# A four-layer graph network kernel: in its second layer, 20 edge tiles of a group are gathered and 5 go by counts, in place of 15 and 10

## The reference, cut to what matters

```python
def _L1_gnn_ref(features, src, dst, W, b):
    out_deg = segment_sum(ones, src); in_deg = segment_sum(ones, dst)
    ci = rsqrt(maximum(out_deg, 1.0)); cj = rsqrt(maximum(in_deg, 1.0))
    msg = features[src] * ci[src][:, None]
    agg = segment_sum(msg, dst) * cj[:, None]
    h = where(in_deg[:, None] > 0, agg, features)
    return relu(h @ W.T + b)
```

## Time and profile before

| | us |
|---|---|
| median of 3 runs | 16802.36 (16799.04 to 16803.32) |
| the profiled execution | 16791.52 |
| its span | 16789.7 |
| `pass1`, from its first body on DVE to its last add | 4280.6 to 7713.2 |
| DVE / POOL / PE busy from 4280 to 7720 | 2392 / 1794 / 2243 of 3440 |
| ACT busy there | 784 |

### The profile page before, as it was taken

How to read it: one execution, slowest core, us unless ns; L and a number is a source line. 1 busy time by engine, 2 the same in 40 slices (tenths; PEclk the granted TensorE clock), 3 DMA queues, 4 the chain that set the end, 5 groups by cost and what they waited for, 6 DMA issues and landing times. The chain is left out here.

```text
span 16789.7 us, 290124 instructions
## 1 busy us (share of the span) xinstructions
PE 11513.4 (69%) x64352; PEld 9568.8 (57%) x64353; DVE 8750.1 (52%) x19588; ACT 3873.3 (23%) x10408; POOL 11073.3 (66%) x11400
## 2 busy tenths in 40 slices
PE   7877877877666666665777766666755446666666
PEld 6777777777444444444555666566643336565555
DVE  4666666666677666664111444444432234444444
ACT  1111111111222222223444211111022223333331
POOL 4777777777545555555666777777546777777773
PEclk9999999999766666665555555555555555555555
DMA  5444444443111111112333333333223333333331
GB/s 130 101 101 101 101 100 101 102 101 91 47 40 43 45 46 44 46 44 76 110 110 110 95 87 87 86 84 90 71 77 92 94 92 95 88 96 92 92 92 51
DMA packets 1579142, 1406.93 MB, mean 84 GB/s; under 512 B 987004, under 2 KB 1445903, under 8 KB 1574658
## 3 DMA queue, kind: packets, MB, share of 16 engines
q1 hardware_dynamic: 601532, 636.68, 14.5%
q0 software_dynamic: 410000, 462.80, 11.0%
q10 hardware_dynamic: 567508, 306.27, 6.6%
HBM read 984.49 MB, written 420.17 MB: 84 GB/s over the span
## 5 line engine op out<-in xcount | busy, mean ns | idle before, releaser
L1757 POOL DMA_INDIRECT order<-l_msg,l_uring x6250 | 6069.5, 971 | 2356.7 <-issue 1831.9
L547 POOL DMA_INDIRECT l_rows<-btab,l_sd x3125 | 2993.7, 958 | 1128.3 <-issue 1087.2
L1906 PEld LDWEIGHTS ps<-l_ordb,l_ohs 128*128 128x128 f32 x15040 | 3263.7, 331 | 313.8 <-issue 313.8
L1906 PE MATMUL ps<-l_ordb,l_ohs 128*128 128x49 f32 x15040 | 3385.3, 415 | 0.0
L1086 POOL DMA_INDIRECT l_rows<-y,l_sd x1875 | 1822.0, 972 | 1621.5 <-DMA l_sd<-in_sd 1087.9
L688 PE MATMUL ps<-l_rhs,l_lhs 64*128 x6250 | 1421.9, 424 | 666.5 <-DVE l_rows L624 466.5
L688 PEld LDWEIGHTS ps<-l_rhs,l_lhs 64*128 64x128 f32 x6250 | 1350.8, 328 | 728.1 <-issue 728.1
L1904 PE MATMUL ps<-l_none 1*128 1x490 bf16 x752 | 438.0, 582 | 1694.4 <-DVE l_ohs L1789 1143.1
L1071 ACT ACTIVATE l_adj<-ps 128x588 f16<-128x588 f32 x1260 | 784.0, 664 | 2636.3 <-PE ps L1315 2629.0
L703 PEld LDWEIGHTS ps<-l_ohe,l_hid 128*128 128x128 f32 x6250 | 1342.8, 332 | 34.7 <-issue 34.0
L703 PE MATMUL ps<-l_ohe,l_hid 128*128 128x32 f32 x6250 | 1359.8, 402 | 0.6 <-ACT l_hid L733 0.6
(11 more groups left out here) (317 smaller groups left out, 15842.4 us busy)
## 6 DMA issues: line engine op xcount, KB each, us to landing
l_ordb<-order SPq DMA_DIRECT2D x752, 250.0 KB
l_dstb<-ids SPq DMA_DIRECT2D x250, 600.0 KB
order<-l_msg,l_uring POOLq DMA_INDIRECT x6250
order<-l_zero ACTq DMA_DIRECT2D x125, 775.0 KB
l_eat<-in_ea40P SPq DMA_DIRECT2D x625, 120.0 KB, 2.1
gates<-l_made ACTq DMA_DIRECT2D x625, 120.0 KB
l_gin<-gates SPq DMA_DIRECT2D x125, 600.0 KB
l_rows<-btab,l_sd POOLq DMA_INDIRECT x3125
```

What stands on the lines that cost most here:

```text
L547: pool.indirect_dma_start(rows[:, t, :], None, d["btab"], bass.IndirectOffsetOnAxis(ap=sd[:, t, 0:1], axis=0)).then_inc(gat[c], 16)
L1757: pool.indirect_dma_start(d["order"], bass.IndirectOffsetOnAxis(ap=uring[:, t:t + 1], axis=0), msg[:, t, :], None).then_inc(sc[c], 16)
L1906: done = t.matmul(red[b % 2][:, ds(slots[k], MW)], ohs[b][:, k, :], ordb[b][:, k, 0:MW], start=False, stop=False, skip_group_check=True)
```

## The change

`SC` goes from 3 to 4, so 20 tiles are gathered and 5 go by counts. The one-hots and builds are laid out anew around the ranking steps: 3 tiles, then the other 2.

```diff
-SC = 3
+SC = 4
 ST = SC * CT
 DT = GT - ST
...
-                    one_hots(0, 4)
+                    one_hots(0, 3)
                     blocks(0)
                     blocks(1)
-                    one_hots(4, 7)
+                    one_hots(3, DT)
                     counts(0)
                     blocks(2)
-                    one_hots(7, 10)
                     counts(1)
                     add_sums(w)
                     blocks(3)
...
-                    build(0, 4)
+                    build(0, 3)
                     before_chunk(0)
-                    build(4, 7)
+                    build(3, DT)
                     behind_chunk(0)
                     before_chunk(1)
-                    build(7, DT)
                     behind_chunk(1)
                     before_chunk(2)
```

## The result

The changed kernel takes 16500.24 us (median of 4 runs, 16497.71 to 16502.51). The ratio to the kernel before is 0.9822, with a 95% interval of 0.9807 to 0.9838: 1.8% faster and clear of no change, as forecast, 23 us under the 16523 and inside the range. The profiled execution took 16502.51 us, against 16791.52 before: -289, where the steps gave -279.

A forecast was written before the change was run, and what follows sets the result against it. The DVE-TensorE chain bounded `pass1`; POOL's gathers would take over. 39 groups at 25.4 us and 84 at 25.35 gave -279 us, 16512.5, plus 10.8 to the median: 16523 us, range 16490 to 16625.

The forecast's parts named there:

- the steps: Summed terms for `pass1`: TensorE's end -277.6 us, four adds behind it -1.1, together -279 us.
- The bound: In `pass1`, POOL's gathers, hidden so far, become the bound: 25.35 us a group against a chain of 24.5 in the last 85.
- The body: Group 17's second body in `pass1` goes, 125 bodies in place of 126: 22.4 us less in the chain.
- The gathers: Twenty gathers a group on POOL, 0.952 us at the median plus 0.305 gap each, taken as 25.35 us a group.
- Landing: From the last gather's end to the use of its rows on TensorE at the end of `pass1`: about 2 us, an estimate.
- The chain: DVE with a piece of TensorE behind the adds: 2.5 us less a body, 27.9 to 25.4 and 27.0 to 24.5.
- the layout: New order of one-hots, builds and count steps: `counts(1)` starts at 5.2 us, not 4.6; wait of 0.6 to 0.7 us.
- the register loads: Five registers fewer for DVE to load at a group's start: gain between 0 and 0.65 us, taken as 0.
- adds and `ohe`: DVE steps in each body: 9 adds in place of 13, -1.13 us; `ohe` of 640 elements, not 480, +0.19 us.
- The columns: `multiply` on TensorE moves half the columns, but weight loads set its spacing of 0.08 us: no gain, -0.
- The two fp32 rows: First-layer 32-column and later-layer 49-column matmuls, same weights, 0.213 and 0.215 us each; taken to show weight loads set the spacing.
- the rival: DVE blocks POOL's gathers: gain eaten at 27.6 us a group; at 29.5 us, 231 us later, 17033 us; chance 3%.

The follow-up runs named there:

- the first eight experiments: Changed kernel: one gather more, five fewer, one DVE step, two fp32 steps; kernel before: five gathers more, one body less, half columns, more register loads; 16400.87 to 16851.39 us.
- the kernel with 15: Kernel before (15 gathers a group) with one further DVE comparison a body, on the slower chip: 24174.59 us, ratio 1.0033 to the kernel before there.

## Why the prediction was right

**The bound.** The chain of DVE and a piece of TensorE, 27 us, gave way to POOL, as laid out: a full gather's price arrives at the end (+157 us), five gathers fewer give back 112 us, and a DVE step gives 9 in place of 84.

**The body.** -22.4 was read, -24.5 measured.

**The gathers.** 25.35 us a group were put; the first wait behind which they run through is at 4308.29 and the last ends at 7416.1, so (7416.1 - 4308.3) / 123 = 25.27. The wait came 2 us later than put (4306.3). 123 x 0.1 = 12 us less and 2 more are the 10 us by which the last gather is early. The mean gather took 959 ns, with fewer one-hots on DVE beside it. Landing took 1.46 us where I estimated 2.

**The chain.** Its saving was mis-sized. I had 2.5 us a body, for 25.4 us in the first 40 groups and 24.5 behind them. The chain by itself, in the changed kernel with 15 gathers, takes 24.4 and 24.0, so 3.5 and 3.0 are saved. One-hots, adds and the layout came out within 0.1 us of the steps (5.19 for 5.2, 5.78 for 5.9, 2.55 for 9 x 0.282). The term that failed is the register loads, "I take 0": 0.50 us of the bound of 0.65. That accounts for the 3.0 behind the first 40 groups. The further 0.5 us within them lie in two other terms. Taken group by group from the traces of before and of the kernel with 15 gathers (groups 2 to 37 without 17), the way from the first one-hot to the first add fell from 7.62 to 5.73 us, 1.9 in place of the 1.6 put, so TensorE showed through with 0.36 us and not 0.65; and the way from there to the reduce fell from 9.69 to 8.64 us, 1.05 where adds and `ohe` had been put at 0.94. It did not move the end, since POOL binds at 25.3 either way; it shows only in how soon POOL has spent its lead: the first 40 groups run at 24.8 us, faster than the gathers, from the lead that they begin with.

**The columns.** -0 was right, by the trace and by the experiment with half the columns. The 0.08 us is the spacing at a granted clock of 0.50 and not at every clock (0.045 us at 1.00). The two fp32 rows could not bear the conclusion: they differ in columns (32 and 49) but also in the granted clock, 1.00 at 1999.74 and 0.50 at 10008.45. Only the experiment changes the columns alone.

**The sum to the median.** The kernel before's profiled execution lay 10.8 us under its median, and I carried that over; after, it lay 2.3 us above. Of the 23 us by which the forecast was high, 13 are this offset and 10 the gathers.

**DVE and the gathers.** That DVE's steps would not make the gathers the slower way was right on the chips of the first eight experiments: their mean stayed at 959 ns. The reading under it was too weak, though. I had "0.2 us and not more" for what a step can cost a gather, while the earlier trace rows already has one of 1325 ns, and the changed kernel has gathers of 1.50 us, held for 0.55 us beside L1179. What kept the rival small is when the gathers start, and not a cap on the price.

**What did not hold everywhere.** The forecast names no chip, and on the slower one the change loses 2.6%. What decides there was not among the rivals: DVE stands still until the group's gathers have been issued. That the gathers cause it rests on where the idle time ends, in all 123 groups, and on what remains of the period without them (15.7 to 16.5 us with 20, 19 and 18); that they alone do is spoken against by the kernel with 15, where DVE often goes on before them. A rival is that DVE's queue gets its next instructions late, since it has no record at all in the long waits; no run tests it. Why it happens on that chip stays open. Open is also whether 19 or 18 gathers win over 20 elsewhere: both were run on the slower chip only. There they only show that fewer gathers are better, and that none of the three beats the kernel before.

## What to carry to other kernels

Before work is moved to an engine that seems idle, sum its instructions with the gap behind each of them: here 76% busy was full. One unit more and one block fewer on the new bound then price it from both sides, and register loads belong in the sum of a chain (0.1 us a register here). A gain that comes from two engines running side by side should be tried on more than one chip: on one of them here it turned into a loss.

## What the hardware showed that was not expected

- The granted clock of the same stretch was 0.66 before, 0.60 with half the columns and nothing else changed, and 0.55 in the changed kernel. TensorE's busy time went up as it fell (by 142 us in the half-column kernel), and the time of the whole did not follow.
- A load of registers costs by their number: 595 ns for 8, 1097 ns for 13.
- The same program took 16812 us on one chip and 24091 on another. The slow one had engine steps and gathers of the usual length, and register steps of 689 ns in place of 85 on DVE and of 698 in place of 29 on SP (medians), and turned the change's -1.8% into +2.6%.
- A DVE step with both inputs in SBUF (L1179) holds a gather that starts inside it until the step ends, less 0.12 us: 0.55 us with 0.67 us of the step left. A reduce and a comparison with one input in PSUM hold it for nothing.
- Matmuls behind weight loads of 96 fp16 columns come 0.08 us apart at a granted clock of 0.50 and 0.045 at 1.00, with 60 and with 30 moving columns alike.
